# The last attention: value products of the chunk one step back between the two turn parts of a chunk

## The chip, the cores and the metric

The kernel runs on one core of one Trainium2 chip. The time is device microseconds of one execution of the whole program. Four compute engines matter here: TensorE (PE, with its weight loads as PEld), VectorE (DVE), ScalarE (ACT) and GpSimd (POOL). Each takes its own list of instructions, and they meet at semaphores.

## The reference, cut to what matters

The program is a four-layer transformer: eight batches of 333 rows (256 tokens of an image and 77 of a text), 256 wide, each layer an attention and a feed-forward part. The change is in the fourth attention: 16 heads of 64, 4 key and value heads, a causal mask with a slope for each head, and a softmax whose sum has 1 added.

```python
att = jnp.einsum('bhqd,bhkd->bhqk', q, k) / np.float32(np.sqrt(D))
att = att + jnp.exp(alibi_log_slopes)[None, :, None, None] * rel[None, None]
att = jnp.where(mask[None, None], att, -jnp.inf)
e = jnp.exp(att - m)
att = e / (1.0 + jnp.sum(e, axis=-1, keepdims=True))
out = jnp.einsum('bhqk,bhkd->bhqd', att, v)
return out.transpose(0, 2, 1, 3).reshape(b, t, H * D) @ Wo
```

Behind it each row is normalised, gets logits for 8 experts, and is sent to the slot of its expert for the last feed-forward part.

## The kernel before, in words

`alibi_attention` (from L2353) runs the last attention. The work is cut into 8 batches, and each batch into 8 chunks (NC = 8) of two heads. The 333 rows are 3 tiles of 111 (TT). All data is 4-byte float. Chunk number u = 8 b + c counts through all batches.

Each engine has a loop over batches and chunks written out by hand, and the order of the instructions in it is the order of the work. In chunk c of a batch:

- **TensorE** (loop from L2984 on): `scores` (L2928) of the chunk two steps ahead into the PSUM tiles l_psA (tiles 0 and 1) and l_psB (tile 2); `turn` part 0 (L2943): six transposes of the finished probabilities of chunk c into l_psP; `turn` part 1: six more, of the last tile of rows, into the same l_psP; `values` (L2959) of the chunk one step back: six products (twelve records of L2966) of the turned probabilities with the values into l_psO.
- Between these stand **pieces**, at three slots of a chunk: slot 0 ahead of turn part 0, slot 1 between the two parts, slot 2 behind part 1. The table `AT` at L2419 gives them by place 3 c + slot. They prepare the next batch (transposes of x, the projections q, k, v) or finish the one before (out: the product with Wo, 8 matmuls, 16 records; rx, rl, rk: the rows, their logits and their ranks). Of the 24 places, 22 are taken. Slot 1 holds x, out, out, out, v, rx, v, v in chunks 0 to 7. All pieces share the PSUM tile l_psM, and each waits until the one before has been copied out. Batch 0 has no pieces of an earlier batch, and the last batch none of a later.
- **VectorE**: the reciprocals of chunk c + 1 (L2709, L2711); the row minima of chunk c + 2 for tiles 0 and 1 (L2704, `rows`); `turned` part 0, two copies of l_psP (L2719, L2720); the minima of tile 2; the copy of a piece if it is one of VectorE's (L2627 for v, L2637 for out); `turned` part 1 (L2722); then, in chunk 3, the statistics of the batch before (L117 to L122), in chunk 4 its normalised rows, in chunk 5 the choice of expert (`route_choose`), in chunk 6 the slots (`route_place`).
- **ScalarE**: `scale_last` of chunk c + 1 (L2805, after the reciprocals); the copy of a piece in slot 0 (L2784 for q, L2781 for rx); the exponentials (L2796) of chunk c + 2, tile 0; `out_turn` of chunk c - 2 (L2810), the copy that empties l_psO; a piece's copy of slot 1; the exponentials of tiles 1 and 2; a piece's copy of slot 2.
- **GpSimd**: `scale` of chunk c, tiles 0 and 1 (L2536, four instructions), after the reciprocals; in chunk 5 the inverse deviation of the batch before, in chunk 6 its plain rows, in chunk 7 its scatter (L2566, three indirect DMAs).

The waits that matter for the order: `turn` part 0 waits for GpSimd's and part 1 for ScalarE's scaled probabilities, and each part waits until the copy of the part before it has emptied l_psP (`pt_done`). `values` waits, at L2960, for both copies of its own chunk, which is the one before, and at L2962 until `out_turn` of the chunk before its own has emptied l_psO:

```python
            def values(b, p, c):
                pe.wait_ge(pt_done, 2 * (NC * b + c) + 2)
                if some(NC * b + c):
                    pe.wait_ge(o_out, NC * b + c)
```

Called with c - 1 in chunk c, it so needs `out_turn` of chunk c - 2, which ScalarE issues in the same chunk c (L2808):

```python
            def out_turn(b, p, c):
                act.wait_ge(pv_done, NC * b + c + 1)
                s_.activation(oT[p][:, c, :], psO[:, 0:T], ACT.Copy).then_inc(o_out, 1)
```

Of the kernel before, what the change touches and what calls it, by code (L numbers as in the profile page):

```python
# [2352 lines left out]
def alibi_attention(nc, sh, ins, routed, stream, xs, out):  # L2353
# [5 lines left out]
    with ExitStack() as ctx:  # L2359
# [68 lines left out]
        def pieces(b, p, c, slot, first, last):  # L2428

            n = N0 if first else 22 * b + 8  # L2430
            for place, kind, j in AT:
                if first and earlier(kind) or last and not earlier(kind):
                    continue
                if place == 3 * c + slot:
                    return [(kind, j, *((b - 1, 1 - p) if earlier(kind) else (b + 1, 1 - p)), n)]
                n += 1
            return []
# [3 lines left out]
        def bank(n):  # L2441

            if isinstance(n, int) and n < N0:
                return first_bank[n % 8]
            if isinstance(n, int) and n >= N_LAST:
                return last_bank[n - N_LAST]
            return psM[:, :]
# [4 lines left out]
        def tail(i):  # L2452
            return *LAST[i], B - 1, 1, N_LAST + i
# [14 lines left out]
        def some(n):  # L2468

            return not isinstance(n, int) or n > 0  # L2470

        def of(b, p, c):

            return (b, p, c) if c < NC else (b + 1, 1 - p, c - NC)
# [383 lines left out]
        def _(pe):  # L2858
            mm = nc.tensor.matmul

            def piece(kind, j, b, p, n):
                if kind == "x" and j == 0:
                    pe.wait_ge(x_in, 32 * b + 32)
                if kind == "out" and j == 0:
                    pe.wait_ge(o_out, NC * b + NC)
                if not isinstance(n, int) or n >= N0:
                    pe.wait_ge(piece_out, n)
                elif n >= 8:
                    pe.wait_ge(piece_out, n - 7)
                if kind == "x":  # L2870
                    for t in range(NT):
                        r = nc.tensor.transpose(bank(n)[:, qt(t)], xn[:, t, 128 * j:128 * j + 128], sh.ident[0:TT, 0:TT])
                if kind == "q":
                    r = mm(bank(n)[:, 0:T], wq[:, 2 * j:2 * j + 2, :, :].rearrange("p h d r -> p (h d r)"), xT[:, 1, :],
                           start=True, stop=True)
                if kind == "k":
                    r = mm(bank(n)[:, 0:T], wk[:, 128 * j:128 * j + 128], xT[:, 1, :], start=True, stop=True)
                if kind == "v":
                    r = mm(bank(n)[0:TT, 0:D], xT[:, 0, qt(j)], wv[:, :], start=True, stop=True)
                if kind == "rx":  # L2880
                    if j == 0:
                        pe.wait_ge(row_ready, b + 1)
                    for t in range(NT):
                        r = nc.tensor.transpose(psM[:, qt(t)], row[:, t, 128 * j:128 * j + 128], sh.ident[0:TT, 0:TT])
                if kind == "rl":
                    for t in range(NT):
                        for k in range(KT):
                            r = mm(psM[0:TT, E * t:E * t + E], rT[:, k, qt(t)], wr[:, k, :],
                                   start=k == 0, stop=k == KT - 1, skip_group_check=True)
                if kind == "rk":  # L2890
                    pe.wait_ge(oh_ready, b + 1)
                    ohf = oh[:, :, :].rearrange("q t e -> q (t e)")
                    mm(bank(n)[0:TT, 0:NT * E], ones[:, :], ohf, start=True, stop=True, skip_group_check=True)
                    r = mm(bank(n)[0:TT, NT * E:2 * NT * E], tri[:, :], ohf, start=True, stop=True, skip_group_check=True)
                if kind == "out":
                    if j == 0:
                        pe.wait_ge(wo_in, 16)
                    for c in range(NC):
                        r = mm(psM[0:TT, 0:D], oT[p][:, c, qt(j)], wo[:, c, :], start=c == 0, stop=c == NC - 1)  # L2899
                r.then_inc(piece_done, 1)  # L2900

            def out_part(p, c0, c1):

                if c0 == 0:
                    pe.wait_ge(min_done, NU * NC * B)
                pe.wait_ge(o_out, NC * (B - 1) + c1)
                for i in range(NT):
                    for c in range(c0, c1):
                        r = mm(last_bank[i][0:TT, 0:D], oT[p][:, c, qt(i)], wo[:, c, :], start=c == 0, stop=c == NC - 1)
                    if c1 == NC:  # L2910
                        r.then_inc(piece_done, 1)
# [16 lines left out]
            def scores(b, p, c):  # L2928

                u = NC * b + c  # L2930
                for t in range(NT):
                    n = TT * (t + 1)
                    if t == 0 and some(u):
                        pe.wait_ge(min_done, NU * u - 2)
                    if t == 2 and some(u):
                        pe.wait_ge(min_done, NU * u)
                    for half in range(2):
                        ph = slice(64 * half, 64 * half + 64)
                        ps = psB[0:TT, half, 0:T] if t == 2 else psA[0:TT, half, at(t):at(t + 1)]
                        mm(ps, qT[p][ph, c, qt(t)], kT[p][ph, c // 4, 0:n],  # L2940
                           start=True, stop=True, skip_group_check=True).then_inc(s_done, 1)

            def turn(b, c, part):  # L2943
                u = NC * b + c
                if part == 0:
                    pe.wait_ge(p_ready, u + 1)
                else:
                    pe.wait_ge(p_last_ready, u + 1)
                if some(2 * u + part):
                    pe.wait_ge(pt_done, 2 * u + part)  # L2950
                blocks = [(0, 0), (1, 0), (1, 1)] if part == 0 else [(2, 0), (2, 1), (2, 2)]
                for half in range(2):
                    for i, (t, a) in enumerate(blocks):
                        r = nc.tensor.transpose(psP[0:TT, half, qt(i)],  # L2954
                                                P[c % 4][:, half, at(t) + TT * a:at(t) + TT * a + TT],
                                                sh.ident[0:TT, 0:TT])
                r.then_inc(t_done, 1)
# [5 lines that stand above are left out]
                for a in range(NT):  # L2963
                    for half in range(2):
                        kv = 2 * (c // 4) + half
                        r = mm(psO[64 * half:64 * half + 64, TT * a:T], vS[p][:, a, DH3 * kv:DH3 * kv + DH3],  # L2966
                               PT[c % 2][:, half, a, TT * a:T], start=a == 0, stop=a == NT - 1, skip_group_check=True)
                r.then_inc(pv_done, 1)
# [15 lines left out]
            def body(b, p, first, last):  # L2984
                for c in range(NC):
                    if c + 2 < NC or not last:
                        scores(*of(b, p, c + 2))
                    for args in pieces(b, p, c, 0, first, last):
                        piece(*args)
                    turn(b, c, 0)  # L2990
                    for args in pieces(b, p, c, 1, first, last):
                        piece(*args)
                    turn(b, c, 1)
                    for args in pieces(b, p, c, 2, first, last):
                        piece(*args)
                    if c > 0:
                        values(b, p, c - 1)
                    elif not first:
                        values(b - 1, 1 - p, NC - 1)
                    if last and c >= NC - 2:  # L3000
                        out_part(p, 0, 4) if c == NC - 2 else out_part(p, 4, 6)
                if last:
                    values(b, p, NC - 1)
                    out_part(p, 6, 7)
                    out_part(p, 7, 8)
                    rows_to_logits()
                    piece(*tail(len(LAST) - 1))
            batches(pe, body)


# [289 lines left out]
```

## Time and profile before

| what | value |
|---|---|
| median of 3 runs | 2106.49 us (2105.95 to 2106.55) |
| the profiled execution: its own time | 2097.64 us |
| its span | 2095.9 us |
| busy over the span: PE | 1792.9 us, 86% |
| DVE | 1117.2 us, 53% |
| ACT | 754.5 us, 36% |
| POOL | 522.2 us, 25% |
| granted clock of TensorE, mean | 0.94 of full speed |
| the chunks of the last attention | about 1389 to 1877 us |

A line of the timeline gives the start in us from the span's start, the duration, the engine, the line of the kernel, the operation, out<-in by the program's names, and the number of instructions merged into it. In brackets stand the idle time of that engine ahead of it and what ended it. Matmuls are pipelined and their ends are modelled, so a following group can start a little before the end shown. The granted clock is the share of full speed that TensorE was given: it has two levels, 1.2 and 2.4 GHz.

### The profile page before, as it was taken

The numbers are of one execution on the slowest core, as the hardware profiler recorded it, in microseconds if no ns is written. First come the engines' busy times: TensorE is split into PE (matmuls) and PEld (weight loads), VectorE is DVE, ScalarE is ACT, GpSimd is POOL, SyncE is SP. The second block draws the span as 40 slices with busy tenths as digits, with TensorE's granted clock in tenths as the row PEclk, the third lists the DMA queues.
The fourth block names the chain that finished last, engine by engine and source line by source line (L and its number), as shares of the span: only waits on it lengthen the run. The fifth ranks groups of instructions, "written<-read, shape, count | busy, mean of one in ns | idle before, by whom it ended". The sixth has DMA issues, their size and how long they took to land. (4 is left out here: it accounts for less than half of the span.)

```text
span 2095.9 us, 32369 instructions
## 1 busy us (share of the span) xinstructions
PE 1792.9 (86%) x9586; PEld 1187.0 (57%) x9586; DVE 1117.2 (53%) x3612; ACT 754.5 (36%) x1859; POOL 522.2 (25%) x710
## 2 busy tenths in 40 slices
PE   3599999987987899788876999779889998884998
PEld 3344444435665677655653767546566666663766
DVE  6477676764245766735552434366666666651111
ACT  1144444442321154322211111066556666631221
POOL 0211000003001122301122333333454445441112
PEclk9899999998997999999987999979999999996999
DMA  5645454509600000081111121070100010003351
GB/s 186 145 95 100 76 101 77 96 1 320 280 0 0 1 1 1 1 328 27 27 35 43 57 65 55 25 186 8 27 21 14 20 28 21 21 20 97 117 168 45
DMA packets 82954, 153.90 MB, mean 73 GB/s; under 512 B 24613, under 2 KB 66484, under 8 KB 78862
## 3 DMA queue, kind: packets, MB, share of 16 engines
q1 hardware_dynamic: 61337, 131.24, 22.8%
q0 software_dynamic: 19712, 18.79, 3.5%
q10 hardware_dynamic: 1764, 2.23, 0.5%
q8 instruction: 58, 0.95, 0.2%
q14 instruction: 83, 0.68, 0.1%
HBM read 90.78 MB, written 64.62 MB: 74 GB/s over the span
## 5 line engine op out<-in xcount | busy, mean ns | idle before, releaser
L2536 POOL TENSOR_SCALAR l_P<-l_P,l_ri 111x111 f32<-111x111 f32 (+1 forms) x256 | 178.0, 714 | 185.9 <-DVE l_ri L2711 185.6
L790 ACT ACTIVATE PT<-psT 111x666 f32<-111x666 f32 x192 | 139.4, 726 | 163.4 <-PE psT L888 163.1
L2796 ACT ACTIVATE l_P<-l_S,l_nm 111x111 f32<-111x111 f32 (+2 forms) x384 | 179.3, 471 | 27.1 <-DVE l_nm L2704 26.9
L687 DVE TENSOR_REDUCE mx<-psS 111x2 f32<-111x666 f32 x192 | 159.6, 847 | 28.0 <-PE psS L873 28.0
L899 PE MATMUL psO<-PT,vS 111*32 111x333 f32 x768 | 147.3, 462 | 0.1
L2954 PE MATMUL l_psP<-ident,l_P 111*111 111x111 f32 x768 | 104.3, 273 | 32.1 <-DVE l_PT L2720 26.0
L2954 PEld LDWEIGHTS l_psP<-ident,l_P 111*111 111x111 f32 x768 | 91.5, 182 | 63.2 <-issue 34.8
L2704 DVE CUSTOM_DVE_ANT_0 l_S<-l_psA,l_am 111x111 f32<-111x111 f32 (+1 forms) x256 | 79.1, 330 | 76.2 <-PE l_psA L2940 68.4
L2299 PE MATMUL t_psH<-expert_w,t_xT 128*128 x224 | 103.1, 605 | 1.5 <-DVE t_xT L2233 1.2
L2322 PE MATMUL t_psY<-expert_w,t_hT 128*128 x448 | 101.7, 380 | 0.7 <-DVE t_yb L2249 0.7
L2177 ACT ACTIVATE t_hg<-t_psH 128x512 f32<-128x512 f32 x56 | 33.5, 598 | 186.6 <-PE t_psH L2299 186.6
L638 POOL TENSOR_TENSOR low<-raw,high 128x333 f32<-128x333 f32 x32 | 28.6, 895 | 275.6 <-DVE high L699 275.6
L2805 ACT ACTIVATE l_P<-l_P,l_ri 111x333 f32<-111x333 f32 x128 | 66.2, 565 | 68.2 <-DVE l_ri L2711 68.2
L2966 PE MATMUL l_psO<-l_PT,l_vS 111*64 111x333 f32 (+2 forms) x768 | 90.1, 371 | 0.0
L2322 PEld LDWEIGHTS t_psY<-expert_w,t_hT 128*128 128x128 f32 x448 | 82.9, 190 | 11.4 <-issue 1.2
L3185 PE MATMUL c_psY<-c_w,c_hT 128*111 128x256 f32 x384 | 84.2, 379 | 0.6 <-DVE c_yb L3132 0.6
L885 PE MATMUL psT<-qs,ks 64*111 64x334 f32 x384 | 79.3, 409 | 4.8 <-DVE mT L715 2.5
L3168 PE MATMUL c_psH<-c_xT,c_w 128*128 128x333 f32 x256 | 76.0, 455 | 8.6 <-DVE c_xT L3115 6.5
L2899 PE MATMUL l_psM<-l_wo,l_oT 128*111 128x256 f32 x336 | 76.5, 381 | 6.9 <-ACT l_oT L2810 6.9
L3132 DVE SCALAR_TENSOR_TENSOR c_yb<-c_psY,c_hb 111x256 f32<-111x256 f32 x24 | 10.2, 424 | 132.7 <-PE c_psY L3185 132.7
L885 PEld LDWEIGHTS psT<-qs,ks 64*111 64x111 f32 x384 | 34.0, 171 | 78.0 <-ACT PT L790 34.7
L2966 PEld LDWEIGHTS l_psO<-l_PT,l_vS 111*64 111x64 f32 x768 | 51.1, 140 | 46.3 <-issue 13.9
(468 smaller groups left out, 3807.2 us busy)
## 6 DMA issues: line engine op xcount, KB each, us to landing
xs_scratch<-zeros SPq DMA_DIRECT2D x30, 896.0 KB, 24.2
expert_w<-in_moe_dram SPq DMA_DIRECT2D x8, 2048.0 KB, 25.5
c_w<-in_moe_dram SPq DMA_DIRECT2D x16, 1024.0 KB, 7.6
qs<-halves_scratch SPq DMA_DIRECT2D x128, 83.5 KB, 3.3
ks<-halves_scratch SPq DMA_DIRECT2D x112, 83.5 KB, 4.1
halves_scratch<-high SPq DMA_DIRECT2D x32, 167.0 KB, 3.2
halves_scratch<-low SPq DMA_DIRECT2D x32, 167.0 KB, 4.1
c_xb<-xs_scratch SPq DMA_DIRECT2D x8, 577.1 KB, 7.3
```

What stands on the lines that cost most here:

```text
L687: v.tensor_reduce(mx[J % 2][:, t, c:c + 65:64], psS[s % 2][0:TT, :, 0:T], AX.X, ALU.max, negate=True).then_inc(max_done, 1)
L790: s_.activation(PT[jp % 2][:, :, a, :], psT[0:TT, :, 0:T], ACT.Exp).then_inc(exp_done, 1)
L885: mm(psT[0:TT, half, 0:TE], ks[p][ph, jp, qt(a)], qs[p][ph, jp, :], start=True, stop=False)
L899: r = mm(psO[at:at + 32, 0:T], vS[p][:, a, h, :], PT[jp % 2][:, half, a, :], start=a == 0, stop=a == NT - 1)
L2299: r = mm(psH[s % 2][q][:, :], xT[s % 2][:, k, :], experts.w[:, e, 1024 * k + 512 * q:1024 * k + 512 * q + 512], start=k == 0, stop=k == KT ...
L2322: r = mm(psY[:, 0:D], hT[s % 2][:, c, :], experts.w[:, e, at:at + D], start=c == 0, stop=c == 7)
L2536: r = g.tensor_scalar(Pt, Pt, ri[:, c % 2, 2 * t + half:2 * t + half + 1], None, ALU.mult)
L2704: v.tensor_tensor_reduce(Sm[:, half, at(t):at(t + 1)], ps, am[:, 2 * c + half, T - n:T], 1.0, BIG, ALU.add, ALU.min, nm[:, c % 2, i:i + 1] ...
L2796: s_.activation(P[c % 4][:, half, at(t):at(t + 1)], Sm[:, half, at(t):at(t + 1)], ACT.Exp, bias=nm[:, c % 2, i:i + 1], scale=-1.0, accum_o ...
L2954: r = nc.tensor.transpose(psP[0:TT, half, qt(i)], P[c % 4][:, half, at(t) + TT * a:at(t) + TT * a + TT], sh.ident[0:TT, 0:TT])
L2966: r = mm(psO[64 * half:64 * half + 64, TT * a:T], vS[p][:, a, DH3 * kv:DH3 * kv + DH3], PT[c % 2][:, half, a, TT * a:T], start=a == 0, sto ...
L3185: r = mm(psY[t % 2][0:TT, 0:D], hT[p][:, f, qt(t)], stream.w[p][:, at:at + D], start=f == 0, stop=f == NF - 1)
```

## The change

In TensorE's loop the call of `values` for the chunk one step back moves from behind slot 2 to ahead of turn part 1, behind the piece of slot 1. In chunk 0 it is the last chunk of the batch before; the very first chunk has none. The lists of the other engines, the buffers, the semaphores and their counts are the same.

```diff
--- before.py
+++ after.py
@@ -2990,13 +2990,13 @@
                     turn(b, c, 0)
                     for args in pieces(b, p, c, 1, first, last):
                         piece(*args)
-                    turn(b, c, 1)
-                    for args in pieces(b, p, c, 2, first, last):
-                        piece(*args)
                     if c > 0:
                         values(b, p, c - 1)
                     elif not first:
                         values(b - 1, 1 - p, NC - 1)
+                    turn(b, c, 1)
+                    for args in pieces(b, p, c, 2, first, last):
+                        piece(*args)
                     if last and c >= NC - 2:
                         out_part(p, 0, 4) if c == NC - 2 else out_part(p, 4, 6)
                 if last:
```

## Rows read from the trace of the kernel before

**Rows 1.** Windows: length; busy us of PE, PEld, DVE, ACT, POOL; clock; DMA share; GB/s.

```profile
1389.00:1877.00 488.00, 437.87 (x3018) 303.71 (x3018) 315.50 (x1321) 302.30 (x1033) 229.23 (x301) 0.97 0.10 28
```

**Rows 2.** Waits, 1389 to 1877 us: who waited for whom, total us, times, longest us.

```profile
PE l_psP L2954 <- DVE l_PT L2720: 26.0, 43, 1.9
...
PEld l_psP L2954 <- DVE l_PT L2720: 15.8, 20, 1.1
...
PE l_psM L2874 <- DVE l_vS L2627: 4.4, 14, 0.3
```

**Rows 3.** Timeline, 1601 to 1611 us: start, duration, what, count, idle before and releaser.

```profile
1601.17 0.75 PE L2954 MATMUL l_psP<-ident,l_P 111*111 111x111 f32 x6
...
1605.14 1.04 ACT L2805 ACTIVATE l_P<-l_P,l_ri 111x333 f32<-111x333 f32 x2 [1.86 <-DVE l_ri L2711]
...
1607.27 0.43 ACT L2810 ACTIVATE l_oT<-l_psO 128x333 f32<-128x333 f32 x1
1607.31 0.38 DVE L2720 COPY l_PT<-l_psP 111x222 f32<-111x222 f32 x1
...
1607.74 0.84 PE L2954 MATMUL l_psP<-ident,l_P 111*111 111x111 f32 x6 [0.37 <-DVE l_PT L2720]
...
1608.92 0.83 PE L2874 MATMUL l_psM<-l_xT,l_wq 128*128 128x333 f32 x2 [0.35 <-DVE l_vS L2627]
...
1609.68 1.35 PE L2966 MATMUL l_psO<-l_PT,l_vS 111*64 111x333 f32 x12
...
1610.96 0.35 PE L2940 MATMUL l_psA<-l_kT,l_qT 64*111 64x111 f32 x2
```

**Rows 4.** Timeline, 1613 to 1636 us, the following turns of batch 3.

```profile
1612.82 0.45 ACT L2781 ACTIVATE l_rT<-l_psM 128x333 f32<-128x333 f32 x1 [0.74 <-PE l_psM L2884]
...
1613.90 0.43 ACT L2810 ACTIVATE l_oT<-l_psO 128x333 f32<-128x333 f32 x1
...
1614.69 0.84 PE L2954 MATMUL l_psP<-ident,l_P 111*111 111x111 f32 x6 [0.87 <-DVE l_PT L2720]
...
1620.00 0.45 ACT L2784 ACTIVATE l_qT<-l_psM 128x333 f32<-128x333 f32 x1 [0.42 <-PE l_psM L2874]
...
1621.08 0.43 ACT L2810 ACTIVATE l_oT<-l_psO 128x333 f32<-128x333 f32 x1
...
1621.56 0.84 PE L2954 MATMUL l_psP<-ident,l_P 111*111 111x111 f32 x6 [0.37 <-DVE l_PT L2720]
...
1628.12 0.43 ACT L2810 ACTIVATE l_oT<-l_psO 128x333 f32<-128x333 f32 x1
...
1634.42 0.83 PE L2954 MATMUL l_psP<-ident,l_P 111*111 111x111 f32 x6 [0.92 <-POOL l_P L2536]
```

**Rows 5.** Timeline of TensorE, 1632 to 1642 us: chunk 0 of batch 4.

```profile
1636.26 0.84 PE L2954 MATMUL l_psP<-ident,l_P 111*111 111x111 f32 x6 [0.72 <-DVE l_PT L2720]
...
1640.86 0.75 PE L2954 MATMUL l_psP<-ident,l_P 111*111 111x111 f32 x6
```

**Rows 6.** Timeline of TensorE, 1500 to 1514 us: chunk 0 of batch 2.

```profile
1503.63 0.83 PE L2954 MATMUL l_psP<-ident,l_P 111*111 111x111 f32 x6 [0.98 <-POOL l_P L2536]
...
1513.20 0.75 PE L2954 MATMUL l_psP<-ident,l_P 111*111 111x111 f32 x6
```

**Rows 7.** Windows view, 1500 to 1520 us.

```profile
1500.00:1520.00 20.00, 17.02 (x100) 11.62 (x96) 8.96 (x35) 10.06 (x35) 8.99 (x13) 0.83 0.20 50
```

**Rows 8.** Timeline, 1397 to 1407 us: chunks 1 and 2 of batch 0.

```profile
1399.16 0.81 PE L2954 MATMUL l_psP<-ident,l_P 111*111 111x111 f32 x6 [1.10 <-DVE l_PT L2720]
...
1403.96 0.43 ACT L2810 ACTIVATE l_oT<-l_psO 128x333 f32<-128x333 f32 x1
...
1405.03 0.81 PE L2954 MATMUL l_psP<-ident,l_P 111*111 111x111 f32 x6 [1.13 <-DVE l_PT L2720]
```

**Rows 9.** Timeline of TensorE, 1844 to 1872 us: chunks 6 and 7 of batch 7.

```profile
1861.69 0.81 PE L2954 MATMUL l_psP<-ident,l_P 111*111 111x111 f32 x6 [1.19 <-DVE l_PT L2720]
...
1871.14 0.81 PE L2954 MATMUL l_psP<-ident,l_P 111*111 111x111 f32 x6 [1.10 <-DVE l_PT L2720]
```

## The prediction

> **What bounds the kernel now.** I first took the stretch of the last attention as a whole: from 1389 to 1877 us TensorE is busy 437.87 of 488 us, VectorE 315.50, ScalarE 302.30, GpSimd 229.23 [rows 1]. TensorE is the fullest engine, but 50 us of it are idle, so I asked what it waits for. The view of the waits says it: before the transposes into l_psP, TensorE and its weight load waited 26.0 + 15.8 = 41.8 us in 63 waits for VectorE's copy at L2720, and before the next piece 4.4 us in 14 waits for the value copy L2627 [rows 2]. These are the waits the change aims at: turn part 1 needs l_psP empty, and stands right behind part 0.
>
> Then I read one whole turn in order of time, chunk 3 to 4 of batch 3 [rows 3]. Call t(c) the start of turn part 1 in chunk c, v(c) the start of the value products issued in chunk c, o(c) the end of ScalarE's L2810 in chunk c, and T(c) the start of turn part 0. Part 1 starts at 1607.74, 0.05 us after L2720 ends (1607.31 + 0.38 = 1607.69). Look at the line above it: L2810 starts at 1607.27 and ends at 1607.70, the same moment. L2810 empties l_psO, and `values` waits for exactly that (L2962). So where the value products are to stand, l_psO comes free no sooner than l_psP does. In chunk 5, o is 1614.33 and t 1614.69; in chunk 6, 1621.51 and 1621.56; in chunk 7, o is 1628.55 [rows 4]. At their old place, 1609.68 [rows 3], the value products never met this wait. It is off today's path and lands on the new one.
>
> **Why L2810 is late.** Its input is old: the products it reads in chunk 5 started at 1609.68 and took 1.35 us, so they ended at 1611.03, and L2810 starts at 1613.90, right after the exponentials ahead of it [rows 3, 4]. The engine takes its instructions in the order of issue: scale of the last rows L2805, the piece's copy, the exponentials of two thirds, then L2810. The Trainium skill, "TensorE: Matmul & The Clock Gate", section "Architectural detail: the array is 16× 32×32, not 1× 128×128", calls the queues of ScalarE and VectorE strictly first in, first out. The row agrees; were it otherwise, L2810 would go at once and the sum would be that of the first rival. L2805 in turn waits for the reciprocal on VectorE (1605.14, released by l_ri L2711), and that stands in VectorE's queue behind the copy L2722 of part 1 and whatever VectorE does for the batch [rows 3].
>
> **The new loop.** With the change, t(c) = v(c) + 1.28, since the value products hold TensorE from 1609.68 to the next scores at 1610.96 [rows 3]. From t(c), L2722, VectorE's batch work, the reciprocal, L2805, the copy and the exponentials lead to o(c+1), and v(c+1) is 0.05 later. Moved ahead of part 1, the 1.28 us of products enter a closed loop; today the loop lacks them. Per turn the loop takes 1.33 plus the return o(c+1) - t(c), from which I subtract what ScalarE idles waiting for TensorE, since TensorE will be early. The return, in batch 3:
> - 3 to 4: 1607.70 - 1601.17 = 6.53 (VectorE does the batch's statistics in it) [rows 3].
> - 4 to 5: 1614.33 - 1607.74 = 6.59, less 0.74 idle before L2781 = 5.85 [rows 3, 4].
> - 5 to 6: 1621.51 - 1614.69 = 6.82, less 0.42 idle before L2784 = 6.40 (the choice of expert in it) [rows 4].
> - 6 to the next batch: the slots are worked out after part 1 of chunk 6, then GpSimd scatters the rows and scales chunk 0, and T(0) waits for that: 1634.42 - 1621.56 = 12.86 [rows 4]. This queue is not passed by the change, it only starts from a later t(6).
>
> Chunks 1 to 3 carry output products between the two parts, which hide both waits, so v(3) falls where t(3) was, 1601.17. Then v(4) = 1601.17 + 1.33 + 6.53 = 1609.03; v(5) = +1.33 + 5.85 = 1616.21; v(6) = +1.33 + 6.40 = 1623.94; T(0) = +1.28 + 12.86 = 1638.08, against 1634.42: **+3.66 us a batch**. TensorE itself doesn't bind: t(4) to t(5) is 6.95 us, less idle times of 0.35 and 0.87 it is 5.73 of work [rows 3, 4], under the 7.18 of the loop.
>
> **The sum.**
> - Batches 1 to 6, six crossings of this stretch: 6 x 3.66 = +22.0.
> - Chunk 0: T(0) comes late, so ScalarE is ahead and l_psO is free in time; part 1 waits 0.72 for the copy [rows 5], and the products fill that wait. Six batches (2 to 7): -4.3.
> - Batch 0: in chunk 1 the first products fill a wait of 1.10 with nothing to wait for: -1.1 [rows 8]. After that, o is 1403.96 + 0.43 = 1404.39 and t 1405.03, 5.87 after the t before it [rows 8]: a turn can gain at most 1405.03 - 1404.39 - 0.05 = 0.59, and loses 0.69 if the whole return of 5.23 is tight (1.33 + 5.23 - 5.87). That return is mostly waiting for scores, so I take -0.2, six times: -1.2.
> - Last batch: part 1 waits in chunk 6 too, 1.19 us [rows 9], so the same loop holds; t(3) to t(6) shift by 1.28 each in turn, 4 x 1.28 = 5.1, less the 1.28 no longer standing behind part 1, less the 1.10 wait of chunk 7 that the products now fill [rows 9]: +2.7.
> - The waits for L2627 (4.4 us) go, but they lie in loop-bound chunks: 0. DMA queues: nothing is moved past them, 0.
>
> Sum: 22.0 - 4.3 - 1.1 - 1.2 + 2.7 = **+18.1 us**. The profiled execution's own time is 2097.64 us for a span of 2095.9; it lies 8.85 under the median 2106.49, so I put the difference on the median: 2106.5 + 18.1 = **2124.6 us**. About 0.2% (4 us) is what a measurement of this kernel can tell from no change.
>
> **Rivals.**
> - The return path has room (faster). Then only what stands at each place counts: o(c) or the end of the piece, whichever is later. Gains 4.3 in the chunks 0, 2.9 in batch 0 (1.10 and three times 0.59), 4.4 for L2627, about 1 elsewhere: -12.6, 2094 us. For it: o and t coincide so closely that the two waits would merely be exchanged. Against: in chunks 4 to 7 VectorE does its batch work between L2722 and the reciprocal, and L2805 starts as soon as L2711 releases it [rows 3]. It decides if the return is shorter than t(c+1) - t(c) less 1.33, that is under about 5.6 us; I read 5.85 to 6.53. Chance 0.12. A full gain of 41.9 + 4.4 us would need l_psO free 0.3 us or more sooner in every chunk, and no row shows it.
> - The clock falls more often (slower still). T(0) to T(1) takes 1640.86 - 1634.42 = 6.44 us in batch 4 [rows 4, 5] and 1513.20 - 1503.63 = 9.57 in batch 2 [rows 6]; the mean granted clock from 1500 to 1520 us is 0.83 [rows 7], so part of it at 1.2 instead of 2.4 GHz. TensorE had stood idle for 0.98 us ahead of that T(0) [rows 6]. In the new kernel TensorE idles 7.18 - 5.73 = 1.4 us and more in each of four chunks. Price: 3.1 us per fall, four further batches 12.5, and up to 6 in the loop: 2137 to 2143 us. Chance 0.22. The same page of the Trainium skill, section "HAM oscillation — how this bites in real kernels", has matmul bursts with waits between them falling to the lower clock again and again; the trace shows it in some batches and not in others with nearly the same waits.
> - The loop closes but is some 3 us a batch looser than I read (the copy and exponentials overlap more), and gains and losses cancel: within 4 us of 2106. Chance 0.05.
>
> The forecast itself has 0.61. The range: below, the loop's returns could be 0.3 us shorter each in 24 turns (-7) and batch 0 could gain 0.59 in each turn (-2.3), with a little more: 2111. Above, the clock case up to 2142. Faster 0.12, same 0.05, slower 0.83.
>
> **What would show it.** In the changed profile: the wait of TensorE for L2720 nearly gone; in its place the first value product in chunks 4 to 7 waits for l_oT L2810, 1 to 2.5 us each, some 30 to 50 us in all; v(4) - v(3) near 7.9 and v(5) - v(4) near 7.2 us; chunk 3 to chunk 0 of the next batch longer by 3 to 4 us, chunks 1 to 3 unchanged. I am wrong if the value products start less than 0.2 us after the piece ahead of them in chunks 5 and 6, or if L2810 ends sooner after t(c) than now.

## The result, and the profile after

The changed kernel takes 2131.27 us (2125.86 to 2137.13, 4 runs) against 2106.22 for the kernel before (2099.73 to 2106.55, 4 runs): ratio 1.0124, interval 1.0103 to 1.0145, so 1.2% slower, 22 to 31 us. The forecast was 2124.6 in a range of 2111 to 2142.

The profiled execution of the changed kernel is the longest of its four, 2137.13 us with a span of 2135.4. Its page: the span, the busy times, and the granted clock in 40 slices.

```profile
span 2135.4 us, 32369 instructions
...
PE 1807.2 (85%) x9586; PEld 1201.1 (56%) x9586; DVE 1113.3 (52%) x3612; ACT 750.1 (35%) x1859; POOL 521.1 (24%) x710
...
PEclk9799999998997999899978999799999999986999
```

Of the 39.5 us by which the two spans differ, 12.5 arise ahead of the changed loop. The first turn part 0 starts at 1402.22 instead of 1389.75 us, in code that is the same; in the runs below it starts between 1392.4 and 1405.1, with the products in either place. I therefore compare the stretch from the first T(0) to the last T(7): 479.55 us before, 508.09 after, **+28.5 us**.

The windows view of that stretch after (columns as in [rows 1]):

```profile
1402.00:1910.00 508.00, 440.79 (x2969) 309.84 (x2968) 309.93 (x1317) 297.67 (x1030) 227.19 (x300) 0.94 0.09 25
```

TensorE is busy 440.79 us where it was 437.87 [rows 1], VectorE, ScalarE and GpSimd a little less than before. The engines do the same work and wait more. The waits view from 1389 to 1920 us says where (who waited for whom, total us, times, longest us), to be held against [rows 2]:

```profile
ACT l_P L2805 <- DVE l_ri L2711: 95.6, 61, 5.2
...
PEld l_psO L2966 <- DVE l_PT L2720: 32.7, 33, 3.4
...
PEld l_psM L2879 <- ACT l_qT L2784: 27.2, 20, 2.0
PE l_psO L2966 <- ACT l_oT L2810: 27.0, 39, 3.2
...
PE l_psM L2879 <- ACT l_qT L2784: 23.6, 18, 1.8
...
PE l_psP L2954 <- DVE l_PT L2720: 0.3, 1, 0.3
```

The waits of the transposes for L2720, 41.8 us before, are down to 0.3. In their place stand 27.0 us of the value products waiting for L2810, and 23.6 us of a value piece (L2879) waiting for ScalarE's copy L2784. The lines of TensorE and of its weight load overlap, so the 27.2 is not added. The view puts another 32.7 us of the products' weight loads down to L2720. The program has no such wait: `values` asks for the copies of the chunk before, which are long done. In the turn below L2720 ends at 1621.45, L2810 at 1621.59, and the weight load starts at 1621.71, so this line is the wait for L2810 once more. ScalarE itself waits 95.6 us for the reciprocal, where it waited 67.7 before.

One turn in order of time, chunks 3 to 5 of batch 3, to be held against [rows 3, 4]:

```profile
1613.82 1.35 PE L2966 MATMUL l_psO<-l_PT,l_vS 111*64 111x333 f32 x12
...
1615.10 0.84 PE L2954 MATMUL l_psP<-ident,l_P 111*111 111x111 f32 x6
...
1615.97 0.85 DVE L2722 COPY l_PT<-l_psP 111x666 f32<-111x666 f32 x1 [1.50 <-PE l_psP L2954]
...
1619.15 1.03 ACT L2805 ACTIVATE l_P<-l_P,l_ri 111x333 f32<-111x333 f32 x2 [2.16 <-DVE l_ri L2711]
...
1621.16 0.43 ACT L2810 ACTIVATE l_oT<-l_psO 128x333 f32<-128x333 f32 x1
...
1621.74 1.35 PE L2966 MATMUL l_psO<-l_PT,l_vS 111*64 111x333 f32 x12 [0.48 <-ACT l_oT L2810]
...
1623.02 0.84 PE L2954 MATMUL l_psP<-ident,l_P 111*111 111x111 f32 x6
...
1628.17 0.43 ACT L2810 ACTIVATE l_oT<-l_psO 128x333 f32<-128x333 f32 x1
...
1628.74 1.35 PE L2966 MATMUL l_psO<-l_PT,l_vS 111*64 111x333 f32 x12 [0.66 <-ACT l_oT L2810]
...
1630.02 0.84 PE L2954 MATMUL l_psP<-ident,l_P 111*111 111x111 f32 x6
```

The chain can be read down the page: products at 1613.82, part 1 at 1615.10, its copy L2722, the batch's statistics, the reciprocal, L2805 at 1619.15, L2810 until 1621.59, and 0.15 us later the next products. VectorE idles 1.50 us ahead of L2722, since the products stand in front of the transposes it waits for. From products to products this is 7.92 us, and 7.00 the next time.

### The profile page after: what moved, and what is told of

Read it like the earlier page. It is cut to its first block and busy times, and to the rows that moved or that the text cites. A ratio compares the mean times of both kernels' runs of the same rounds, so it can differ in the third digit from the quotient of the medians.

```text
span 2135.4 us, 32369 instructions
## 1 busy us (share of the span) xinstructions
PE 1807.2 (85%) x9586; PEld 1201.1 (56%) x9586; DVE 1113.3 (52%) x3612; ACT 750.1 (35%) x1859; POOL 521.1 (24%) x710
## 5 line engine op out<-in xcount | busy, mean ns | idle before, releaser
L2536 POOL TENSOR_SCALAR l_P<-l_P,l_ri 111x111 f32<-111x111 f32 (+1 forms) x256 | 177.5, 710 | 208.8 <-DVE l_ri L2711 208.5
L2966 PE MATMUL l_psO<-l_PT,l_vS 111*64 111x333 f32 (+2 forms) x768 | 96.0, 388 | 27.6 <-ACT l_oT L2810 27.0
L2954 PE MATMUL l_psP<-ident,l_P 111*111 111x111 f32 x768 | 111.3, 285 | 0.3 <-DVE l_PT L2720 0.3
L2722 DVE COPY l_PT<-l_psP 111x666 f32<-111x666 f32 x64 | 54.5, 852 | 106.6 <-PE l_psP L2954 106.6
L2805 ACT ACTIVATE l_P<-l_P,l_ri 111x333 f32<-111x333 f32 x128 | 66.2, 565 | 95.6 <-DVE l_ri L2711 95.6
L2966 PEld LDWEIGHTS l_psO<-l_PT,l_vS 111*64 111x64 f32 x768 | 60.0, 147 | 69.0 <-DVE l_PT L2720 32.7
```

Of the source, the lines that this page charges most:

```text
L2536: r = g.tensor_scalar(Pt, Pt, ri[:, c % 2, 2 * t + half:2 * t + half + 1], None, ALU.mult)
L2954: r = nc.tensor.transpose(psP[0:TT, half, qt(i)], P[c % 4][:, half, at(t) + TT * a:at(t) + TT * a + TT], sh.ident[0:TT, 0:TT])
```

## The experiments

Each number is a median with the ratio to the kernel before on the same chip. The stretch is the one from the first T(0) to the last T(7) of the profiled execution.

**e1: L2810 first on ScalarE, in the changed kernel.**

```diff
 # scalar engine, body of the chunk loop
+                    if c >= 2:
+                        out_turn(b, p, c - 2)
+                    elif not first:
+                        out_turn(b - 1, 1 - p, NC + c - 2)
                     if c + 1 < NC or not last:
                         scale_last(*of(b, p, c + 1)[::2])
...
                     if new:
                         exps(b2, c2, 0)
-                    if c >= 2:
-                        out_turn(b, p, c - 2)
-                    elif not first:
-                        out_turn(b - 1, 1 - p, NC + c - 2)
```

> The changed kernel, with ScalarE's copy L2810 (out_turn) as the first thing of a chunk, ahead of the scale L2805, the piece's copy and the exponentials. Loop theory (the 1.28 us of products got into a loop of copy L2722, VectorE's batch work, reciprocal, L2805, exponentials, L2810): the 27.0 us that the products wait for L2810 in the changed kernel go, but the second way through the same engines stays, reciprocal, L2805, piece's copy L2784, next piece (18 waits of 23.6 us in the changed kernel), so about 25 us under the changed kernel and within 8 us of the kernel before: 2098 to 2108 us. Clock theory (the loss is TensorE at the lower clock, whatever it waits for): under 10 us of gain, 2121 us or more. Theory of place (products ahead of part 1 cost time by themselves): no gain, 2131 us.

Measured: 2091.44 us, ratio 0.9935 (0.9913 to 0.9958), 40 us under the changed kernel. One instruction takes another place on ScalarE, and the change turns from a loss into a gain. It gave more than I expected, and one reason is that L2810 was also what the first output piece waited for, 8.2 + 3.9 us in the changed kernel. The waits that are gone, 27.0 + 12.1 = 39.1 us, come near the 40; how much of it is clock that came back, no run separates. The waits of e1 in the same stretch:

```profile
PEld l_psM L2879 <- ACT l_qT L2784: 27.2, 20, 2.0
...
PE l_psM L2879 <- ACT l_qT L2784: 23.7, 18, 1.8
...
PE l_psP L2954 <- DVE l_PT L2720: 2.7, 2, 1.9
```

The wait for L2810 is gone and the wait for L2784 is whole: the second path is a real one, and it is what keeps e1 from more. This counts against the clock theory as the main cause and against the theory of place.

**e2: the same edit in the kernel before.**

> The kernel before, with only L2810 as the first thing of a chunk. Control for what the earlier copy gives by itself. Loop theory: the products of the old order never waited for L2810, so the gain is only the wait of the first out piece for it, 6.9 + 2.4 us in the kernel before: 2096 to 2100 us. If the early copy delays L2805 and the exponentials on a path that ends last, 2106 us or more.

Measured: 2096.24 us, ratio 0.9965 (0.995 to 0.998), as expected: 7 to 9 us, the wait of the output piece. So of e1's 40 us some 7 to 9 have nothing to do with the products' place, and with L2810 first the products' new place is worth 0.3%, about 6 us.

**e3: L2810 first, L2805 behind the piece's copy of slot 0, products in the new place.**

```diff
 # scalar engine, body of the chunk loop, on top of e1
-                    if c + 1 < NC or not last:
-                        scale_last(*of(b, p, c + 1)[::2])
                     b2, _, c2 = of(b, p, c + 2)
                     new = c + 2 < NC or not last
                     for args in pieces(b, p, c, 0, first, last):
                         piece(*args)
+                    if c + 1 < NC or not last:
+                        scale_last(*of(b, p, c + 1)[::2])
```

> The changed kernel, with L2810 first and L2805 behind the piece's copy of slot 0. Loop theory: both ways from the products back to the products are cut (L2810 and L2784 no longer stand behind the reciprocal), so the wait for L2720 of the kernel before (41.8 us) is filled and nothing takes its place but the wait for GpSimd in chunk 0: 15 to 30 us under the kernel before, 2076 to 2091 us. Clock theory: about as the kernel before at best, 2106 us. Theory of place: 2125 us or more.

Measured: 2080.70 us, ratio 0.9873 (0.985 to 0.9895), 25 us under the kernel before by medians and 27 by the ratio, stretch 449.91 us. Both paths had to be cut. What TensorE still waits for in the transposes:

```profile
PE l_psP L2954 <- POOL l_P L2536: 11.7, 5, 2.8
...
PE l_psP L2954 <- DVE l_PT L2720: 9.5, 16, 1.9
...
PEld l_psP L2954 <- POOL l_P L2536: 8.2, 3, 3.4
...
PEld l_psP L2954 <- DVE l_PT L2720: 6.6, 10, 0.8
```

**e4: the products moved in chunks 0 to 3 only.**

```diff
-                    if c > 0:
+                    if (c < 4) and c > 0:
                         values(b, p, c - 1)
-                    elif not first:
+                    elif (c < 4) and not first:
                         values(b - 1, 1 - p, NC - 1)
                     turn(b, c, 1)
                     for args in pieces(b, p, c, 2, first, last):
                         piece(*args)
+                    if not (c < 4) and c > 0:
+                        values(b, p, c - 1)
+                    elif not (c < 4) and not first:
+                        values(b - 1, 1 - p, NC - 1)
```

> The products ahead of part 1 in chunks 0 to 3 only; in chunks 4 to 7 behind slot 2, as before. Loop theory: chunks 1 to 3 have output products between the parts and close no loop, chunk 0 gains 0.7 us a batch; -5 to +2 us against the kernel before, 2101 to 2108 us. Theory of place: half of the loss stays, 2119 us.

Measured: 2107.95 us, ratio 1.002 (0.9999 to 1.0041). No gain and hardly a loss; the single runs spread further than elsewhere, from 2097.89 to 2121.1 us.

**e7: the other half, chunks 4 to 7 only** (the same edit with c >= 4).

> The products ahead of part 1 in chunks 4 to 7 only (e4 is the other half). Loop theory: the loss sits here, 3 to 4 us a batch, without the gain of chunk 0 and batch 0's first chunks: 2122 to 2134 us. Theory of place: half of the loss, 2119 us.

Measured: 2126.94 us, ratio 1.0101 (1.0082 to 1.012). Nearly the whole loss sits in the four chunks in which no output piece stands between the parts. That excludes the theory of place.

**e5: control for e3, products in the old place, ScalarE ordered as in e3.**

> The products in their old place, ScalarE as in e3: L2810 first, L2805 behind the piece's copy of slot 0. Control for e3. Loop theory: with the old order the products are in no loop, the 41.8 us of waits for L2720 stay, so this is about e2, 2093 to 2101 us, and the move of the products is worth some 15 to 20 us of e3's gain. If e3's gain is ScalarE's order alone: 2077 to 2084 us.

Measured: 2105.67 us, ratio 0.9999 (0.9983 to 1.0016). The expectation missed by 5 us: the later L2805 cost the 9 us that the earlier L2810 gave. The waits show it:

```profile
PE l_psP L2954 <- DVE l_PT L2720: 29.1, 43, 1.9
...
PEld l_psP L2954 <- DVE l_PT L2720: 17.6, 20, 1.1
...
PEld l_psP L2954 <- ACT l_P L2805: 13.8, 15, 1.4
```

In the old order part 1 comes so soon that it now waits 13.8 us for L2805. In the new order the products stand ahead of it and give L2805 that time. On ScalarE's order of e3 the products' new place is worth 25 us (2105.67 to 2080.70).

**e6: only L2805 moved, behind the exponentials and L2810, in the changed kernel.**

```diff
 # scalar engine, body of the chunk loop
-                    if c + 1 < NC or not last:
-                        scale_last(*of(b, p, c + 1)[::2])
...
                         out_turn(b - 1, 1 - p, NC + c - 2)
+                    if c + 1 < NC or not last:
+                        scale_last(*of(b, p, c + 1)[::2])
```

> The changed kernel, with only L2805 moved: behind the exponentials and L2810, which keep their order. The reciprocal is then no longer ahead of L2810 or L2784; the exponentials still wait for the minima, which stand behind L2722 on VectorE. Loop theory: the return loses L2805's 1.04 us (and 1.33 + 6.53 falls to about 6.8), so most of the 25 us go: 2100 to 2112 us. Theory that L2810 has only to come first: 2125 us or more.

Measured: 2106.24 us, ratio 0.9996 (0.9982 to 1.0011). As expected, the return got shorter and the loss of 25 us was gone. From products to products in batch 3 it is 7.09 us (6.8 expected) and then 6.49, instead of 7.92 and 7.00. The edit also cuts the second path: TensorE's waits for L2784, 23.6 us in the changed kernel, are gone, so e6 does not separate the two paths. The loop is still there, with less in it, and as L2784 no longer holds TensorE ahead of the products, their wait for L2810 is no shorter in sum:

```profile
PE l_psO L2966 <- ACT l_oT L2810: 29.6, 31, 2.7
...
PE l_psP L2954 <- POOL l_P L2536: 10.9, 5, 2.6
```

**e9: VectorE's batch work ahead of L2722, in the changed kernel.**

```diff
 # vector engine, body of the chunk loop
+                    if c == 3 and not first:
+                        dve.drain()
+                        batch_stats(nc, dve, sh, b - 1).then_inc(h_done, 1)
+                    if c == 4 and not first:
+                        route_rows(b - 1)
                     turned(b, c, 1)
                     for args in pieces(b, p, c, 2, first, last):
                         piece(*args)
-                    if c == 3 and not first:
-                        dve.drain()
-                        batch_stats(nc, dve, sh, b - 1).then_inc(h_done, 1)
-                    if c == 4 and not first:
-                        route_rows(b - 1)
```

> The changed kernel, with VectorE's statistics (chunk 3, 1.8 us) and normalised rows (chunk 4, about 0.95 us) ahead of the copy L2722 instead of behind it. VectorE idles there for the products and the transposes, so they leave the return and fill that wait. Loop theory: a turn 3 to 4 takes 7.9 us less about 1.7, a turn 4 to 5 7.0 less about 0.8, so 2.5 us a batch, seven batches: 17 us under the changed kernel, about 2114 us (2108 to 2120). If VectorE's work is not in the path that ends last, 2131 us.

Measured: 2107.30 us, ratio 1.0013 (1.0 to 1.0026), 24 us under the changed kernel. This is the direct test of the loop: ScalarE's and TensorE's lists are untouched, and VectorE does the same work, most of it in the time in which it idled. Chunks 3 to 5 of batch 4 in e9:

```profile
1665.26 1.35 PE L2966 MATMUL l_psO<-l_PT,l_vS 111*64 111x333 f32 x12
...
1666.01 1.08 DVE L117 BATCH_NORM_STATS2 moments<-h 111x6 f32 x3
...
1666.54 0.84 PE L2954 MATMUL l_psP<-ident,l_P 111*111 111x111 f32 x6
...
1667.76 0.85 DVE L2722 COPY l_PT<-l_psP 111x666 f32<-111x666 f32 x1
...
1668.99 1.04 ACT L2805 ACTIVATE l_P<-l_P,l_ri 111x333 f32<-111x333 f32 x2 [0.55 <-DVE l_ri L2711]
...
1671.15 0.43 ACT L2810 ACTIVATE l_oT<-l_psO 128x333 f32<-128x333 f32 x1
...
1671.73 1.35 PE L2966 MATMUL l_psO<-l_PT,l_vS 111*64 111x333 f32 x12 [0.47 <-ACT l_oT L2810]
...
1677.87 1.35 PE L2966 MATMUL l_psO<-l_PT,l_vS 111*64 111x333 f32 x12 [0.65 <-ACT l_oT L2810]
```

Products to products took 7.92 and 7.00 us in the changed kernel; here 1671.73 - 1665.26 = 6.47 and 1677.87 - 1671.73 = 6.14. Batch 3 of e9 shows the same, 6.47 and 6.15. That is 2.3 us a batch, 16 in seven, close to the 17 expected. Over all seven batches the two turns got shorter by more, 22.0 us (t(3) to t(5), in sum 109.36 us in the changed kernel and 87.33 in e9): in batches 1, 4, 5 and 7 of the changed kernel the products of chunk 4 take 1.82 to 2.49 us instead of 1.35 and part 1 behind them 1.46 instead of 0.84, the lower clock, and in e9 they do so in none. In the profiled execution the mean granted clock of the stretch is 0.98 (windows view, columns as in [rows 1]) where it was 0.94, so shorter waits probably bring back clock as well; that part is read from one execution and not separated by a run. Nor was the same edit made with the products in their old place, so that all of e9's gain belongs to the loop is read from the turns and not shown by a control.

```profile
1400.00:1875.00 475.00, 420.40 (x2951) 295.56 (x2951) 307.43 (x1302) 295.69 (x1018) 223.01 (x295) 0.98 0.09 25
```

**e8: e3, with GpSimd's scale of the next batch's chunk 0 ahead of the scatter.**

```diff
 # gpsimd, body of the chunk loop
-                    scale(b, c)
+                    if c > 0 or first:
+                        scale(b, c)
                     if c == 6 and not first:
                         row_rest(b - 1)
+                    if c == 7 and not last:
+                        scale(b + 1, 0)
                     if c == 7 and not first:
                         scatter(b - 1)
```

> e3, with GpSimd scaling chunk 0 of the next batch ahead of the scatter in chunk 7 (it stood behind it). In e3 turn part 0 of chunk 0 still waits 11.7 + 8.2 us for L2536. If that wait ends last there, 8 to 20 us under e3: 2061 to 2073 us. If VectorE or ScalarE are as late, or the scatter now delays the scale of chunk 1: within 4 us of e3, 2077 to 2085 us.

Measured: 2063.00 us, ratio 0.9797 (0.9776 to 0.9817). That is 18 us under e3. The wait for L2536 was the next one in line: 11.7 and 8.2 us in e3 (TensorE and its weight load), 1.2 and 1.8 in e8.

**e11: control for e8, products in the old place, L2810 first.**

> The products in their old place, with L2810 first on ScalarE and GpSimd's scale of chunk 0 ahead of the scatter. Control for e8: with the old order the waits for L2720 stay. e2 (2096 us) less the wait for GpSimd in chunk 0, 0.9 us in six batches, of which the wait for L2720 behind it stays: 2088 to 2094 us, and so the products' new place is worth some 25 us once the other engines' order allows it. If 2066 us or less, the new place is worth nothing.

Measured: 2083.80 us, ratio 0.9909 (0.9891 to 0.9926), some 4 us better than expected. Against e2 the scale ahead of the scatter gives 12 us here; I had counted only 0.9 us for six batches. Against e8 the products' new place is worth 21 us.

**e10: e8 with e9's order on VectorE.**

> e8, with the same two steps ahead of L2722. In e8 the products no longer close the loop, and part 1 waits for nothing; the copy L2723 in front of part 0 or 1 still holds TensorE 16 us. If part 1's scale or the scores are still led by VectorE in chunks 3 and 4: up to 6 us under e8, 2057 to 2060 us. If the loop is fully cut: as e8, 2061 to 2065 us.

Measured: **2053.35 us**, ratio 0.9766 (0.9747 to 0.9784), the best of all. Against e8 that is 10 us by medians, 6.5 by ratios, at or over the top of what I expected. The waits for the copy of part 0 (here L2723) are down to 9.8 us, from 41.8 in the kernel before and 16.2 in e8:

```profile
PE l_psP L2957 <- DVE l_PT L2723: 6.0, 10, 1.4
...
PEld l_psP L2957 <- DVE l_PT L2723: 3.8, 6, 0.8
```

## Why the prediction was right

The direction, the size within its range and the mechanism hold. The terms of the sum hold less well. From trace to trace the six crossings gave +31.4 for +22.0, chunk 0 of batches 2 to 7 -10.7 for -4.3, batch 0 -2.7 for -2.3, chunks 1 to 7 of the last batch +11.2 for +2.7; with -0.7 elsewhere that makes the 28.5. The two large misses carry falls of the clock, which the sum had at nothing, and what stood against them in chunk 0 came for another reason than the forecast's. That the sum came within 7 us of the median is partly luck. Point by point:

- **The turn of the loop.** Products to products in batch 3: 7.86 forecast and 7.92 measured for 3 to 4, 7.18 and 7.00 for 4 to 5, 7.73 and 7.72 for 5 to 6 (1636.46 - 1628.74). The one constant that was off is the step from L2810 to the products: 0.15 us instead of 0.05, as 1621.59 to 1621.74 shows.
- **T(0) of the next batch.** Forecast 3.66 us later per batch, measured 4.81 in batch 3: from v(3) at 1613.82 to T(0) at 1651.88 are 38.06 us, against 33.25 before (1601.17 to 1634.42). The rows of TensorE around it:

```profile
1636.46 1.35 PE L2966 MATMUL l_psO<-l_PT,l_vS 111*64 111x333 f32 x12 [0.48 <-ACT l_oT L2810]
1637.74 0.84 PE L2954 MATMUL l_psP<-ident,l_P 111*111 111x111 f32 x6
...
1643.55 0.78 PE L2879 MATMUL l_psM<-l_wv,l_xT 128*111 128x256 f32 x2 [1.81 <-ACT l_qT L2784]
1644.71 2.49 PE L2966 MATMUL l_psO<-l_PT,l_vS 111*64 111x333 f32 x12 [0.39 <-ACT l_oT L2810]
1647.13 1.46 PE L2954 MATMUL l_psP<-ident,l_P 111*111 111x111 f32 x6
...
1651.88 0.75 PE L2954 MATMUL l_psP<-ident,l_P 111*111 111x111 f32 x6
...
1653.74 1.35 PE L2966 MATMUL l_psO<-l_PT,l_vS 111*64 111x333 f32 x12 [0.65 <-ACT l_oT L2810]
```

  The products at 1644.71 take 2.49 us instead of 1.35, and part 1 behind them 1.46 instead of 0.84: TensorE runs there at the lower of its two clocks, after idle times of 1.81 and 0.39 us. So TensorE, not GpSimd, sets this T(0): part 1 of chunk 6 to T(0) takes 14.14 us instead of 12.86. Over the six batches the term was +22.0; measured from trace to trace it is +31.4, which also holds an idle time of 3.7 us at the head of the loop body in batch 3 (t(6) to T(0) 16.60 us instead of 12.85).
- **Chunk 0: -4.3 forecast, which failed.** I had written that l_psO is free in time there. The last line above shows the products waiting 0.65 us for L2810 in chunk 0 as well, in place of the 0.72 for L2720. T(0) to T(1) is 1658.34 - 1651.88 = 6.46 us, against 6.44. The gain is nil; the slack ScalarE had before was the time in which T(0) waited for GpSimd, and it was gone when TensorE came late itself. e4 shows that the gain is there where T(0) is not late: in its batch 6 chunk 0 takes 5.65 us instead of 6.51. It is lost again from chunk 3 on, and the batch takes 60.94 us against 60.97. Only in batches 2, 3 and 7, where chunk 0 held a fall of the clock or the idle head of the loop body before [rows 6, 7], it is 3.1 to 4.4 us shorter after, 10.7 us together. In batch 3 that is mostly the idle time that moved into the crossing. In batches 2 and 7 the fall now comes in chunk 7 ahead, where it cost nothing: t(6) to T(0) is 12.86 and 12.59 us, 12.91 and 12.65 before.
- **A path I did not list.** L2784 also stands behind L2805 and holds the value piece L2879, 23.6 us. Where both paths come back to the same products the turn is no longer than by L2810 alone, so the sum was not hurt. One sign failed with it: I had forecast waits for L2810 of 1 to 2.5 us each and 30 to 50 in all, and they are 0.7 on average and 27.0 in all, since most of TensorE's idle time stands ahead of L2879. For the remedy the second path counts: e1 cut one of them and left the other.
- **Batch 0.** Forecast -2.3, measured 47.79 us from its first T(0) to the next batch's, against 50.46: -2.7.
- **The last batch.** Forecast +2.7, measured +11.2 over its chunks 1 to 7 (T(1) to T(7) 54.60 us, 43.43 before). The loop is there as forecast, but with idle times of 3.23 and 2.65 us the clock falls, and the output products behind it, sixteen records, take 5.40 us where they took 3.71:

```profile
1884.12 2.49 PE L2966 MATMUL l_psO<-l_PT,l_vS 111*64 111x333 f32 x12 [3.23 <-ACT l_oT L2810]
...
1899.50 2.03 PE L2966 MATMUL l_psO<-l_PT,l_vS 111*64 111x333 f32 x12 [2.65 <-ACT l_oT L2810]
...
1903.34 5.40 PE L2909 MATMUL l_psA<-l_wo,l_oT 128*111 128x256 f32 x16
...
1910.31 0.75 PE L2954 MATMUL l_psP<-ident,l_P 111*111 111x111 f32 x6
```

- **The clock.** The second rival is partly true. Forecast with its 3.1 us a fall it was to give 2137 to 2143 us; the runs lie from 2125.86 to 2137.13, between the two cases. In the kernel before, the falls came in chunk 0 of batches 2, 3 and 7 [rows 6, 7] and in chunk 5 of batch 1; after, they come at the products of chunk 7 in batches 1 to 6, of chunk 4 in batches 1, 4, 5 and 7, and of chunk 6 in batch 7. Up to batch 6 each follows a wait of L2879 for L2784 of 1.25 to 1.81 us and one of the products for L2810 of 0.34 to 0.48, in the last batch one for L2810 of 3.23 and of 2.65 us. Nearly the same waits brought a fall in batch 1 and none in batch 3:

```profile
1485.11 0.68 PE L2879 MATMUL l_psM<-l_wv,l_xT 128*111 128x256 f32 x2 [1.41 <-ACT l_qT L2784]
1486.27 1.82 PE L2966 MATMUL l_psO<-l_PT,l_vS 111*64 111x333 f32 x12 [0.48 <-ACT l_oT L2810]
...
1620.57 0.69 PE L2879 MATMUL l_psM<-l_wv,l_xT 128*111 128x256 f32 x2 [1.40 <-ACT l_qT L2784]
```

  The Trainium skill, "TensorE: Matmul & The Clock Gate", section "HAM oscillation — how this bites in real kernels", has a kernel whose clock falls again after each wait between bursts of matmuls. The trace agrees with the pattern, but its waits are shorter than the DMA waits of that case. The falls hang on the loop: e6 and e9 leave TensorE's order alone, shorten the return, and the whole 25 us go. In e9's trace those of chunk 4 are gone, and three of the six of chunk 7 are left.
- **The first rival**, room in the return, is refuted by e9: with VectorE's batch work out of the return, the turns get shorter by 1.45 and 0.86 us. There was no room.

What stays open: how the 25 us divide between the loop and the clock over many executions. By batch 3 the loop alone gives (4.81 - 1.28) x 6 = 21.2 (1.28 is 14.14 - 12.86, the part at the lower clock), less 2.7 for batch 0: some two thirds of the stretch's 28.5 us. No run held the clock still.

## What to carry to other kernels

Before filling a wait with work from elsewhere, look up what that work waits for itself, and read in the profile when that comes free: here the copies of two engines ended within 0.01 us of each other in the turn that I read, so one wait was only exchanged for another. Then ask whether the moved work now stands ahead of something that its own release depends on; if so its duration is added to every turn of a loop, even though the engine that does it has idle time. The same move was worth 25 us the other way once ScalarE took the emptying copy first and the scale later: an order on one engine can only be judged together with the orders of the others.

## What the runs showed of the hardware

The clock fell after idle times of TensorE of 1.81 and 0.39 us close together, and of 2.65 and 3.23 us, and the fall comes on top of the wait: in the last batch 5.40 - 3.71 = 1.69 us on one group of output products. Nearly the same waits did not bring a fall in every batch: after 1.41 and 0.48 us the products took 1.82 us in batch 1, after 1.40 and 0.48 they took 1.35 in batch 3. The start of the changed stage, in code that all kernels share, moved by up to 15 us between executions (1389.75 to 1405.13 us), more than the effect of some of the edits; a profile's span alone would have read the change as 39.5 us.
